# Spreading per-token factors in an attention and mixture-of-experts kernel: bf16 parts, a broadcast transfer, and steps cut into pieces

## What is computed

```python
h = tok_ref(x, W)                              # (8, 1024, 64)
h = concatenate([h, txt], axis=1)              # (8, 1056, 64)
h = h + attn(layernorm(h))                     # 4 heads of 16, softmax over 1056 keys
h = h + ffn(layernorm(h))                      # 8 experts, top 2 of a softmax gate, gelu

def layernorm(x): return (x - mean(x)) / sqrt(var(x) + 1e-5)
def attn(x):
    q, k, v = heads(x @ w_qkv.T)
    p = softmax(q @ k.T * 16**-0.5)
    return (p @ v) @ w_proj.T + b_proj
```

## Time and profile before

| | us |
|---|---|
| median of 3 executions (997.33 to 1000.4) | 999.66 |
| the profiled execution | 1001.97 |
| its span in the trace | 1000.2 |
| PE busy (matmuls) | 899.0 |
| DVE busy | 573.0 |
| ACT busy | 494.4 |
| POOL busy | 138.7 |
| prologue and first maxima, until the first shifted scores | 108 |
| slots 0 to 7, until the last heads are copied | 108 to 739 |
| epilogue | 739 to 758 |
| phase 2 | 759 to 1000 |

### The profile page before, as it was taken

One profiled execution on the slowest core, in us unless ns is written; L12 is line 12 of the kernel. 1 busy time (PEld: TensorE's weight loads), 2 busy tenths in 40 slices (PEclk: granted clock), 3 DMA queues, 4 the chain that ended last, 5 costly groups with the idle time before them and its releaser, 6 DMA issues. The chain is left out here.

```text
span 1000.2 us, 17890 instructions
## 1 busy us (share of the span) xinstructions
PE 899.0 (90%) x5900; PEld 374.9 (37%) x5900; DVE 573.0 (57%) x1201; ACT 494.4 (49%) x1189; POOL 138.7 (14%) x148
## 2 busy tenths in 40 slices
PE   5665899999999989999999999999965989899996
PEld 5241322433342343343243334333412535354443
DVE  4025565578874557876557887788230553636331
ACT  0020254466664536665446676666533454555552
POOL 0010100011010011101001101001000344444443
PEclk9965589899999988999989999999876999999998
DMA  8329351027551005536002305100006655382731
GB/s 153 57 47 163 62 62 31 3 35 119 97 69 44 2 4 67 117 67 110 2 1 30 40 2 68 44 3 1 1 5 141 120 126 117 80 184 52 155 78 22
DMA packets 55864, 64.58 MB, mean 65 GB/s; under 512 B 23893, under 2 KB 41825, under 8 KB 55777
## 3 DMA queue, kind: packets, MB, share of 16 engines
q1 hardware_dynamic: 55777, 63.46, 35.5%
HBM read 36.73 MB, written 2.43 MB: 39 GB/s over the span
## 5 line engine op out<-in xcount | busy, mean ns | idle before, releaser
L887 DVE TENSOR_REDUCE max_parts<-bank 128x1 f32<-128x512 f32 x512 | 329.6, 685 | 137.4 <-PE bank L1075 134.5
L811 ACT ACTIVATE probs<-bank 128x384 f32<-128x384 f32 (+1 forms) x768 | 313.4, 466 | 191.1 <-PE bank L1038 189.6
L1038 PE MATMUL bank<-q_stack,k_stack 99*128 99x384 bf16 (+1 forms) x768 | 229.9, 329 | 4.9 <-ACT probs L811 4.2
L1075 PE MATMUL bank<-k_stack,q_stack 96*128 96x512 bf16 x512 | 208.4, 409 | 17.2 <-DMA k_stack<-part 13.2
L1016 PE MATMUL bank<-probs,v_tiles 128*32 128x384 f32 (+1 forms) x1536 | 160.2, 490 | 5.4 <-ACT heads_out L796 5.0
L1038 PEld LDWEIGHTS bank<-q_stack,k_stack 99*128 99x128 bf16 x768 | 72.2, 99 | 196.1 <-ACT probs L811 146.1
L1285 ACT ACTIVATE hid<-bank,biases 128x352 f32<-128x352 f32 x192 | 96.0, 552 | 84.8 <-PE bank L1329 84.7
L1304 DVE SCALAR_TENSOR_TENSOR prod<-bank,biases,cwb 128x352 f32<-128x352 f32 x96 | 55.8, 582 | 120.1 <-PE bank L1317 103.0
L1329 PE MATMUL bank<-x,w 128*128 128x352 bf16 (+1 forms) x576 | 105.2, 320 | 6.3 <-DMA x<-part 6.3
L1317 PE MATMUL bank<-hid,w_sb 128*64 128x352 f32 x384 | 79.2, 491 | 7.7 <-DVE prod L1304 4.0
L1052 PE MATMUL bank<-x,tok_m 128*64 128x512 f32 x256 | 68.5, 634 | 9.4 <-DMA text_in<-in_txt 8.0
(11 more groups left out here) (146 smaller groups left out, 704.2 us busy)
## 6 DMA issues: line engine op xcount, KB each, us to landing
cwb<-gates_by_expert SPq DMA_DIRECT2D x16, 1056.0 KB, 12.1
x<-in_x SPq DMA_DIRECT2D x64, 256.0 KB, 6.9
q_stack<-part SPq DMA_DIRECT2D x48, 132.0 KB, 6.1
k_stack<-part SPq DMA_DIRECT2D x48, 132.0 KB, 6.6
x<-part SPq DMA_DIRECT2D x32, 132.0 KB, 2.5
h_res<-h_new SPq DMA_DIRECT2D x4, 528.0 KB, 3.0
h_all<-h_res SPq DMA_DIRECT2D x4, 528.0 KB, 3.1
h<-h_all SPq DMA_DIRECT2D x8, 264.0 KB, 3.2
```

What stands on the lines that cost most here:

```text
L811: nc.scalar.activation(probs[:, group % 3, h, 0:n], src, ACT.Exp, scale=SCALE).then_inc(exp_done, 1)
L887: nc.vector.tensor_reduce(max_parts[:, c, H * j + h, i % 2:i % 2 + 1], src[:, :], AX.X, ALU.max)\
L1038: last = nc.tensor.matmul(bank[:, 0:n], ks[par][0:ROWS + 3, h, P * kt:P * kt + P], qs[par][0:ROWS + 3, h, QC[qc]], start=True, stop=True)
L1075: last = nc.tensor.matmul(bank[:, :], queries(h, j), ks[par][0:ROWS, h, HALF * (i % 2):HALF * (i % 2) + HALF], start=True, stop=True)
```

## The change

1. The inverse roots are cut into three bf16 parts (`split_roots`, four more dependent DVE instructions), and `spread_roots` adds them up with 18 bf16 matmuls for each third of the tokens in place of 6 fp32 ones.
2. The reciprocals are spread by a DMA: a third transfer at unit 0 of a slot waits for `recip_moved` and copies each of the 4 rows of `recip_rows`, now rows 0 to 3, to 32 rows of `recip` (128 rows of 4224 bytes). The selecting matmuls and ACT's copies are gone. POOL multiplies in a step `normalise` that waits for `recip_spread`, and the projections stand at units 23, 26 and 29.
3. The maxima are cut into bf16 parts ahead of the transposing matmul: DVE writes them once and splits them with four dependent instructions; the matmul is bf16, and after it DVE makes one copy in place of four instructions.
4. In the tokenising slots the variances stand at units 76, 77 and 78, three tiles at each; the first guess of the roots at 78, the Newton steps at 79, 80 and 81, the split at 82 and the spreading at 83, 85 and 87; `project` in these slots moves one unit back.

The diff, cut to its core:

```diff
-AT_FINISH = [17, 20, 23, 26, 29, 32]
+AT_NORMALISE = [20, 23, 26]
+AT_FINISH = [23, 26, 29]
-AT_TOKENISE = [AT_EMBED[0][-1], AT_EMBED[1][-1], 65, 68, 71, 74, 77, 80, 82, 84]
-AT_PROJECT = {"odd": [34, 37, 40], "even": [89, 92, 95]}
+AT_VARY = [76, 77, 78]
+AT_ROOT = [79, 80, 81, 82]
+AT_TOKENISE = [AT_EMBED[0][-1], AT_EMBED[1][-1], 65, 68, 71, 74, AT_VARY[-1], 83, 85, 87]
+AT_PROJECT = {"odd": [34, 37, 40], "even": [90, 93, 96]}
...
+        def split_roots(dve, done, n):
+            t, y = root_work[:, 1, :], roots[:, :]
+            step = ROOT_STEPS * n + 13
+            dve.wait_ge(done, step)
+            nc.vector.tensor_copy(root_part[:, 0, :], y).then_inc(done, 1)
+            dve.wait_ge(done, step + 1)
+            nc.vector.tensor_tensor(t, y, root_part[:, 0, :], ALU.subtract).then_inc(done, 1)
+            dve.wait_ge(done, step + 2)
+            nc.vector.tensor_copy(root_part[:, 1, :], t).then_inc(done, 1)
+            dve.wait_ge(done, step + 3)
+            return nc.vector.tensor_tensor(root_part[:, 2, :], t, root_part[:, 1, :], ALU.subtract)
...
-                for bp in range(2):
-                    last = nc.tensor.matmul(bank[D * bp:D * bp + D, tokens.start - WIDE * i:tokens.stop - WIDE * i],
-                                            roots[0:n, 2 * t + bp:2 * t + bp + 1].broadcast_to([n, D]),
-                                            ident[0:n, 0:n], start=True, stop=True)
+                for part in range(3):
+                    for bp in range(2):
+                        col = 2 * t + bp
+                        last = nc.tensor.matmul(bank[D * bp:D * bp + D, tokens.start - WIDE * i:tokens.stop - WIDE * i],
+                                                root_part[0:n, part, col:col + 1].broadcast_to([n, D]),
+                                                ident_half[0:n, 0:n], start=(part == 0), stop=(part == 2),
+                                                skip_group_check=True)
...
+                    elif (stage, i) == ("spread", 1):
                         sp.wait_ge(recip_done, t + 1)
-                        sp.dma_start(recip_rows[DH:P:32, :], den[:, :]).then_inc(recip_moved, 16)
+                        sp.dma_start(recip_rows[:, :], den[:, :]).then_inc(recip_moved, 16)
+                    elif stage == "spread":
+                        sp.wait_ge(recip_moved, 16 * (t + 1))
+                        sp.dma_start(recip[:, :], recip_rows[:, :].unsqueeze(1).broadcast_to([H, 32, L]))\
+                          .then_inc(recip_spread, 16)
...
-                    elif stage == "finish" and i % 2 == 0:
-                        freed(pool, i, g)
+                    elif stage == "normalise":
+                        pool.wait_ge(recip_spread, 16 * (t + 1))
+                        pool.wait_ge(side_free, g)
...
+                            dve.wait_ge(neg_step, step + 1)
+                            nc.vector.tensor_copy(neg_part[:, kinds, :, 0, :], negm[:, kinds, :, :]).then_inc(neg_step, 1)
+                            dve.wait_ge(neg_step, step + 2)
+                            nc.vector.tensor_tensor(neg_rest[:, kinds, :, :], negm[:, kinds, :, :],
+                                                    neg_part[:, kinds, :, 0, :], ALU.subtract).then_inc(neg_step, 1)
...
+                        nc.vector.tensor_copy(m_part[:, :], max_bank[place][0:3 * QR, 0:P]).then_inc(max_done, 1)
...
-                        if i == 0:
-                            pe.wait_ge(recip_moved, 16 * (t + 1))
-                        if i % 2 == 0:
-                            last = nc.tensor.matmul(bank[:, 0:CH], den_sel, recip_rows[:, chunk[c]], start=True, stop=True)
-                        else:
-                            pe.wait_ge(on_ready, NCH * t + c + 1)
-                            last = nc.tensor.matmul(bank[rows, 0:CH], projT[:, :], on[:, chunk[c]], start=True, stop=True)
+                        pe.wait_ge(on_ready, NCH * t + i + 1)
+                        last = nc.tensor.matmul(bank[rows, 0:CH], projT[:, :], on[:, chunk[i]], start=True, stop=True)
```

More of the change, by code:

```diff
@@ L112 @@
 N_FFN = 8
-PRESETS = 21
-USES = {"tokenise": 10, "project": 3, "values": 2, "finish": 6}
+PRESETS = 22
+USES = {"tokenise": 10, "project": 3, "values": 2, "finish": 3}
 def build(nc, x, txt, tok_w, w_qkv, w_proj, b_proj, gate_w, gate_b, w1, b1, w2, b2, consts, out):
@@ L287, in side_steps @@
             if u == 0 and "finish" in stages:
-                for i in range(2):
+                for i in range(3):
                     order.append(("spread", i, b - 1, 1 - par, q, g))
@@ L355, in run_phase1 @@
                     side("embed", (i, j), None, None, 0, 0)
+                for j in range(2 if i == 6 else 0):
+                    side("vary", j, None, None, 0, 0)
                 side("tokenise", i, None, None, 0, 0)
+                for j in range(4 if i == 6 else 0):
+                    side("root", 1 + j, None, None, 0, 0)
             for i in range(USES["project"]):
@@ L431, in build, with token_variances @@
         wide = [slice(WIDE * i, min(WIDE * i + WIDE, L)) for i in range(NCH)]
-        def token_variances(bank, squares):
-            for t, tokens in enumerate(NORM_TILES):
+        def token_variances(bank, squares, part):
+            for t in range(3 * part, 3 * part + 3):
+                tokens = NORM_TILES[t]
                 rows = slice(0, tokens.stop - tokens.start)
@@ L616, in norm_tensor @@
             elif name == "roots":
-                last = token_variances(bank, sq)
+                for part in range(3):
+                    last = token_variances(bank, sq, part)
             elif name == "scale":
-                last = spread_roots(bank, roots, i)
+                last = spread_roots(bank, i)
             elif name == "gates":
@@ L898, in side @@
                             dve.wait_ge(max_done, at + 1)
-                            for n in range(3):
-                                last = nc.vector.tensor_reduce(negm[:, c // 2, 0:nt, n, :], parts[:, 0:nt, :, :], AX.X,
-                                                               ALU.max, negate=True)
+                            step = 4 * (NCH * t + c)
+                            kinds = slice(0, 1) if c < NCH - 1 else slice(1, 3)
+                            last = nc.vector.tensor_reduce(negm[:, kinds.start, 0:nt, :], parts[:, 0:nt, :, :], AX.X,
+                                                           ALU.max, negate=True)
                             if c == NCH - 1:
```

163 lines of the change are left out of this document (87 added, 76 removed).

## The result

The changed kernel takes 1172.9 us (median of 4 executions, 1171.1 to 1175.5) against 998.5 us for the kernel before (4 executions): 1.174 times, 95% interval 1.170 to 1.178. It is slower by 174 us. The forecast was 1163 with a range of 1005 to 1195; sign and likeliest mechanism were right.

The account below looks back on a forecast made before the run. PE sets the pace, DVE next; 1002.0 + 138 (broadcast's delays) + 16 - 11 - 4.8 - 1.4 + 4.8 + 8.4 + 1.7 + 11.1 = 1164.8, with the profiled execution 2.3 above the median: 1163 us, range 1005 to 1195.

Parts of the forecast that it names:

- likeliest mechanism: Slots and epilogue: slow broadcast out of four partitions holds up PE and the stack; 1135 to 1195 us, chance 0.57.
- The broadcast's landing, 20 us: Broadcast of reciprocals: four source partitions at 7.5 GB/s each, 30 GB/s, 18 us of data and 20 to the landing.
- The rival of few engines: Broadcast dealt to 4 of 16 DMA engines: 104 GB/s, 7.0 us to the landing, 1062 us in all; chance 0.10.
- First wait 16, second wait, delay 21 a slot: Slot 5: PE waits 16 us at unit 23 for the broadcast, then at unit 33 behind the stack; delay 21 together.
- 138 + 16 - 11 = 143: Slots 1 to 7: broadcast's delays +138, low clock +16, selecting matmuls saved -11.
- The clock, +16: Low granted clock behind PE's waits: 2 us in each of six slots and 4 in slot 7, +16.
- Transpositions, -4.8: 24 transpositions of maxima lose three of four passes, about 0.2 us each; -4.8, bounds 0 and 6.
- Spreading in bf16, +4.8: Roots: 18 bf16 matmuls take 0.95 us where six fp32 took 0.76, +0.2 for each of 24; +4.8.
- Pieces, +8.4: Roots in three tokenising slots: PE waits 3.6 us for DVE's pieces, 1.0 before; 2.8 each, +8.4.
- +10 for the three parts: Everything but the broadcast part: transpositions -4.8, bf16 spreading +4.8, pieces +8.4, prologue, slot 7 and phase 2 +1.7.
- Epilogue, +11.1: Epilogue: 14.2 us before, 25.3 after with 20.0 for the broadcast; +11.1.
- Prologue and phase 2: Small costs outside the slots: prologue +0.5 us, phase 2 +0.3 us, where PE has its own work meanwhile.

Follow-up runs that it names:

- the kernel with selecting matmuls: The changed kernel without its second part: reciprocals spread by selecting matmuls and ACT's copies again, the other parts kept; 1009.1 us, 1.009.
- the kernel with four transfers: The changed kernel with the broadcast cut into four transfers, one for each head, rows still neighbours; 1169.7 us, 1.167.

## Why the prediction was right, point by point

**What bounds the kernel.** Right in the main: PE time removed comes off slots 0 to 6 for the most part (3.2 of the 4.2 forecast for part 3, in one execution each). In slot 7 it does not, as doubted.

**The broadcast's landing, 20 us.** Too short by 3 alone (23.2 from issue to POOL's start in the epilogue) and by 5 with the stack (24.8 to 25.2). The rate is 25 GB/s, not 30. The bound was taken from a transfer that is narrow at its target; that it bore on a narrow source was the weak point named, and it held to a fifth. There is luck in that: the working went by the number of partitions, 7.5 GB/s for each, and four rows four apart moved 81 GB/s, where it gives the same 30. It came out because the rows, like the stack's bands, are neighbours. The Trainium skill's figure (SBUF — State Buffer, "Door 1: The DMA port swizzle"), 27.6 GB/s for one port, lies nearer to the 25 measured; and moving the rows to partitions that it puts on ports of their own gave 81. The Trainium skill's rule on the number of engines (DMA: Bandwidth & Descriptors, "Why a DMA increments its semaphore by 16 and not by 1") agrees too: share 0.24 for a slowest dimension of 4, about 1.0 for 32.

**The rival of few engines.** Half true, and it was priced as an alternative. Four engines do carry the transfer (by the share of 0.24), but they don't set its rate while the rows are neighbours; with the rows apart the stack behind them costs 11.6 us (20.3 against 8.7), and four shared engines are the likeliest reason, not a shown one.

**First wait 16, second wait, delay 21 a slot.** The first wait was mis-sized: 21.3, 21.3, 20.3, 21.3, 21.3, 21.0 and, without a stack, 19.0 us. The second, forecast as the difference of some 5, was at most 1.5 us. PE was later than supposed and ran at the low clock behind the wait, so it reached unit 33 at R+39.0 in slot 5, and the shift's transfers, forecast for R+36, let it start at R+39.5 (633.21 to 672.72). So the delay of a slot came near 21 because one wait was 5 us too small and the other up to 5 too large. Against the kernel with selecting matmuls slots 1 to 7 are 22.8, 21.4, 21.9, 21.9, 22.4, 22.2 and 18.4 us longer, together 151; the same terms gave 138 + 16 - 11 = 143.

**The clock, +16.** First and second waits come to 149 in the slots; less 12 of selecting matmuls that leaves about 14 for the clock, a remainder that no run measures by itself.

**Transpositions, -4.8.** Near in slots 0 to 6 (-3.2) and wrong in sum, for a wait that the working passed over: the split was counted as lying under PE "while DVE has those 12 us". That is an average over a slot, and the one place where PE has nothing else, the last chunk of slot 7, is most of what turned -4.8 into +6.

**Spreading in bf16, +4.8.** Wrong in sign for PE alone: 18 bf16 matmuls are recorded with 0.67 to 0.70 us at the full clock where 12 fp32 records took 0.82 to 0.84 (compare), and 1.17 against 1.55 at the low one. I streamed 128 columns each instead of taking the lower bound of 0.7 that the 32-column row gave. **Pieces, +8.4.** PE waits 2.8 us for the split in each of the three slots, not 3.6:

```profile
193.55 1.17 PE L505 MATMUL bank<-ident_half,root_part 128*64 128x128 bf16 x18 [2.80 <-DVE root_part L495]
```

Parts 1 and 4 together cost 4 us by the medians, forecast 13 to 15. So +10 for the three parts was right by errors that cancel. How the 2 and 2 us divide stays open; both lie within the intervals.

**Epilogue, +11.1.** Measured +14.8; the landing's 3 us are most of the difference (the terms listed there add up to 25.5, not 25.3). **Prologue and phase 2** (+0.5, +0.3) moved -0.9 and -2.1, within what the prologue (105.7 to 108.1 us) and the rest of the span behind the epilogue (240 to 245 us) differ by between these kernels.

## What to carry to other kernels

A transfer that replaces matmuls must be priced by where its rows lie and by the queue behind it: here 528 KB from four neighbouring partitions took 23 us until their first use, from four partitions four apart 8.7, from device memory 4.2 to 5.3 (reciprocals at unit 8), and even then the transfers behind it cost more than the matmuls had. When a dependent step is moved, look for the one place where the waiting engine has no other work; a share of busy time over the whole slot says nothing about it. A short wait of PE can cost several times its length in the clock behind it (1.95 us, and a chunk 6 us longer), and moving one step by two units can take it back.

## What the runs showed of the hardware

- Rate by source, for the same bytes and the same target: partitions 0 to 3, 25 GB/s with 4 or with 16 DMA engines; partitions 0, 4, 8, 12, 81 GB/s with 4 engines.
- The busy share of the DMA engines does not follow their rate: 1.04 at 30 GB/s in the kernel with four transfers, against 1.03 at 204 GB/s in phase 2 of the changed kernel (window below). A full share is no sign of a full rate.
- A queue that is jammed holds the issuing engine too: SP's issues of the stack took 4.0 to 4.4 us each behind the broadcast, 0.6 before.
- PE's idle time of 2.06 us (last transposition) and of 1.95 (unit 33 of slot 5) were followed by a granted clock of 0.50 or near it for up to 10 us of full work; at the same places 1.40, 0.85 and none were not, nor was 1.66 at the first projection of slot 5. The length of the wait does not settle it: behind 2.74 us at unit 33 of slot 1 the clock was 0.71 for 5 us and then 0.95.

```profile
940.00:944.00 4.00, 4.00 (x20) 1.67 (x17) 0.00 (x0) 2.02 (x6) 0.00 (x0) 0.97 1.03 204
```
